# An attention and mixture-of-experts block: zeros multiplied on TensorE at the start, first loads reordered over two queues, a shorter first tile table, the last row copy issued later

## The reference

```
Q, K, V = x @ W_Q, x @ W_K, x @ W_V
x  = layernorm(x + softmax(causal(Q K^T / sqrt(128))) V)
logits = (x @ gate_w + gate_b) / 0.9 ; keep the best 2 of 8 ; p = softmax over those 2
h  = gelu(x @ w1[e] + b1[e]) ; y = sum over the 2 experts of p * (h @ w2[e] + b2[e])
x  = layernorm(x + (layernorm(y) * ln_g + ln_b))
```

## Time and profile before

| | us |
|---|---|
| median of 3 runs | 262.4 (260.68 to 263.1) |
| the profiled execution | 262.94 |
| its span in the trace | 261.1 |
| TensorE busy | 231.4 (89% of the span) |
| ScalarE busy | 179.9 (69%) |
| VectorE busy | 173.8 (67%) |
| GpSimd busy | 144.9 (55%) |
| mean granted TensorE clock | 0.963 of full |
| chain that ended last: TensorE, ScalarE, VectorE | 70%, 13%, 7% |

### The profile page before, as it was taken

How to read it: one execution, slowest core, us unless ns; L and a number is a source line. 1 busy time by engine, 2 the same in 40 slices (tenths; PEclk the granted TensorE clock), 3 DMA queues, 4 the chain that set the end, 5 groups by cost and what they waited for, 6 DMA issues and landing times.

```text
span 261.1 us, 7284 instructions
## 1 busy us (share of the span) xinstructions
PE 231.4 (89%) x1867; PEld 211.8 (81%) x1868; DVE 173.8 (67%) x957; ACT 179.9 (69%) x527; POOL 144.9 (55%) x165
## 2 busy tenths in 40 slices
PE   2789899899999899989999999999999999999200
PEld 2547687787887799989999999999999999999100
DVE  0043768688888878556883333355568989899984
ACT  2355675687784879968877655665566897589962
POOL 8300004727777777777877777766544445555600
PEclk9999999999999979999999999999999999999755
DMA  4999210221221345441527797768689775834266
GB/s 126 257 324 330 57 43 23 91 62 55 91 92 54 82 131 139 119 129 53 124 74 213 230 313 212 247 195 238 197 250 357 240 206 169 258 137 122 80 207 166
DMA packets 45105, 42.38 MB, mean 162 GB/s; under 512 B 5488, under 2 KB 34080, under 8 KB 45072
## 3 DMA queue, kind: packets, MB, share of 16 engines
q1 hardware_dynamic: 40752, 33.10, 44.4%
q0 software_dynamic: 4320, 8.92, 9.8%
HBM read 27.89 MB, written 12.01 MB: 153 GB/s over the span
## 4 chain that ended last, share of the span: by engine, by line
PE 70%; ACT 13%; DVE 7%; issue 3%; DMA 2%; DVEq 2%; SPq 1%; ACTq 1%
PE bank L584 21%; PE bank L573 21%; PE bank L434 6%; PE bank L461 6%; ACT h L737 4%; PE bank L420 3%; PE bank L501 3%; PE bank L449 2%; ACT pair L742 2%; PE bank L425 2%; PE bank L482 2%; ACT probs L665 2%; ACT rows L657 2%; DMA slot_x<-slots 2%; PE bank L581 1%
## 5 line engine op out<-in xcount | busy, mean ns | idle before, releaser
L737 ACT ACTIVATE h<-bank,b_cols 128x128 f32<-128x128 f32 x284 | 81.9, 383 | 38.3 <-PE bank L573 37.9
L1322 POOL DMA_INDIRECT slots<-rows,slot_of x64 | 65.4, 1022 | 57.1 <-DVE rows L972 38.8
L1327 POOL DMA_INDIRECT returned<-x,slot_back x71 | 71.4, 1006 | 44.4 <-DVE x L1107 35.2
L584 PE MATMUL bank<-w_all,h 128*128 x568 | 78.5, 282 | 0.0
L573 PE MATMUL bank<-slot_xT,w_now 128*128 128x128 f32 x568 | 75.0, 275 | 0.0
L584 PEld LDWEIGHTS bank<-w_all,h 128*128 128x128 f32 x568 | 69.0, 192 | 0.8
L573 PEld LDWEIGHTS bank<-slot_xT,w_now 128*128 128x128 f32 x568 | 69.1, 192 | 0.1
L869 DVE CAST slot_back<-slot_x 128x1 uint32<-128x1 f32 x71 | 10.4, 146 | 39.5 <-PE bank L573 39.5
L826 DVE TENSOR_REDUCE negmax<-bank 128x1 f32<-128x128 f32 (+3 forms) x32 | 14.7, 484 | 20.4 <-PE bank L435 19.9
L461 PEld LDWEIGHTS bank<-v,probsT 128*128 128x128 f32 x160 | 20.3, 198 | 5.7 <-issue 3.8
L1107 DVE TENSOR_SCALAR x<-bank,slot_gate 128x128 f32<-128x128 f32 x71 | 24.0, 341 | 0.0
(11 more groups left out here) (152 smaller groups left out, 305.5 us busy)
## 6 DMA issues: line engine op xcount, KB each, us to landing
w_now<-in_L_ffn_w_dram SPq DMA_DIRECT2D x47, 256.0 KB
slot_x<-slots SPq DMA_DIRECT2D x71, 65.0 KB
w_all<-in_L_ffn_w_dram SPq DMA_DIRECT2D x16, 256.0 KB, 5.8
pair<-returned SPq DMA_DIRECT2D x14, 256.0 KB, 4.2
x<-n_L_attn_embeddings_dram SPq DMA_DIRECT2D x8, 256.0 KB, 4.2
rows<-rows SPq DMA_DIRECT2D x8, 256.0 KB, 2.8
returned<-x,slot_back POOLq DMA_INDIRECT x71, 3.1
slots<-rows,slot_of POOLq DMA_INDIRECT x64, 2.3
```

The costliest lines, as they stand in the source:

```text
L584: m = nc.tensor.matmul(o, h[:, s % RING, c * P:(c + 1) * P], w2_c, start=False, stop=(c == FC - 1))
L737: m = nc.scalar.activation(h[:, s % RING, cols], bank_[:, cols], ACT.Gelu, bias=b1_cols[:, c:][:, bass.ds(first, 1)])
L1322: g_.indirect_dma_start(slots, bass.IndirectOffsetOnAxis(ap=slot_of[:, b, c:c + 1], axis=0), rows[:, k, b * TB + t, :], None).then_inc(dis ...
L1327: g_.indirect_dma_start(returned, bass.IndirectOffsetOnAxis(ap=slot_back[:, j:j + 1], axis=0), y[:, j % Y_RING, :], None).then_inc(y_retur ...
```

## The change

- A tile `idle` of 128 x 512 bf16 is set to zero as VectorE's first instruction. TensorE multiplies it (`stay_awake`, 128 x 128 by 512 columns) five times before its first wait for data, once after the m matmul and once after batch 0's projection. The products go to a bank that is written over later.
- x of batch 0 is issued from ScalarE's queue, as its first instruction. wq and wk are SyncE's first two DMAs. wv has a semaphore of its own, and TensorE waits for it only before the values of batch 0.
- ScalarE copies xT of batch 0 before mqk.
- Three operations on `taken` (one partition, eight numbers) move from the first table to the second.
- `copy_rows(7)` is issued after the load of slot 13 in place of slot 10.

```diff
+        idle = sb("idle", [P, 512], BF16)
...
-        w_loaded = sem("w_loaded")
+        idle_ready = sem("idle_ready")
+        w_loaded, wv_loaded = sem("w_loaded"), sem("wv_loaded")
...
-            load_x(0)
             sp.dma_start(wq[:], W_Q).then_inc(w_loaded, 16)
             sp.dma_start(wk[:], W_K).then_inc(w_loaded, 16)
-            sp.dma_start(wv[:], W_V).then_inc(w_loaded, 16)
+            sp.dma_start(wv[:], W_V).then_inc(wv_loaded, 16)
             load_x(1)
...
-                    if j == UNROLL + AHEAD - 1:
+                    if j == UNROLL + AHEAD + 2:
                         copy_rows(B - 1)
...
+            def stay_awake(n):
+
+                for _ in range(n):
+                    nc.tensor.matmul(T0[:], idle[:, 0:P], idle[:], start=True, stop=True)
+
+            pe.wait_ge(idle_ready, 1)
+            stay_awake(5)
             pe.wait_ge(const_ready, FIRST_CONST)
-            pe.wait_ge(w_loaded, 48)
+            pe.wait_ge(w_loaded, 32)
             nc.tensor.transpose(A1[:, 0:P], wq[:], ident[:])
             nc.tensor.transpose(A1[:, P:2 * P], wk[:], ident[:]).then_inc(wT_psum, 1)
             transpose_x(0)
             pe.wait_ge(wT_ready, 1)
             nc.tensor.matmul(A1[:, 2 * P:3 * P], wqkT[:, 0:P], wqkT[:, P:2 * P], start=True, stop=True).then_inc(m_psum, 1)
+            stay_awake(1)
             pe.wait_ge(m_ready, 1)
             project_g(0)
+            stay_awake(1)
+            pe.wait_ge(wv_loaded, 16)
             project_v(0)
...
+            act.dma_start(x[:, 0:TB, :], emb[0].rearrange("(t p) d -> p t d", p=P)).then_inc(x_loaded[0], 16)
             act.wait_ge(ones_ready, 1)
             nc.scalar.activation(egap[:, 0:1], ones[:, 0:1], ACT.Exp)
             act.wait_ge(wT_psum, 1)
             nc.scalar.activation(wqkT[:], A1[:, 0:2 * P], ACT.Copy).then_inc(wT_ready, 1)
+            copy_xT(0)
             act.wait_ge(m_psum, 1)
             nc.scalar.activation(mqk[:], A1[:, 2 * P:3 * P], ACT.Copy, scale=SCALE).then_inc(m_ready, 1)
-            copy_xT(0)
...
                 elif q == 4:
                     vec.tensor_tensor(some, tiles_by(FULL, E), by_tiles(ends[:, 0:E], FULL, E), ALU.is_ge)
-                    vec.tensor_tensor(taken[:], full[:], ends[:, 0:E], ALU.subtract)
                 elif q == 5:
                     vec.tensor_tensor(some, some, by_tiles(skip[:, 0:E], FULL, E), ALU.mult)
-                    vec.tensor_scalar(taken[:], taken[:], float(FULL * P), 0.0, ALU.add, ALU.max)
                 elif q == 6:
                     vec.tensor_reduce(steps[:, 0:FULL], some, AX.X, ALU.add)
-                    vec.tensor_tensor(taken[:], taken[:], full[:], ALU.min)
...
                     vec.tensor_copy(pad_at[:], running[0:1, B % 2, :]).then_inc(pads_known, 1)
+                    vec.tensor_tensor(taken[:], full[:], ends[:, 0:E], ALU.subtract)
...
                     vec.tensor_scalar(up_i[:], up[:], float(P - 1), None, ALU.add)
+                    vec.tensor_scalar(taken[:], taken[:], float(FULL * P), 0.0, ALU.add, ALU.max)
...
                     vec.tensor_scalar(up_i[:], up_i[:], -P, None, ALU.bitwise_and)
+                    vec.tensor_tensor(taken[:], taken[:], full[:], ALU.min)
...
+            vec.memset(idle[:], 0.0).then_inc(idle_ready, 1)
             vec.memset(both[:], 0.0)
```

## The result

| | before | changed |
|---|---|---|
| median of the runs compared | 262.75 us (260.68 to 265.95, 4 runs) | 257.81 us (257.17 to 258.35, 4 runs) |
| ratio | | 0.9847, interval 0.9804 to 0.9889 |
| profiled execution | 262.94 us, span 261.1 | 257.17 us, span 255.4 |

The ratio on record is estimated from fast executions alone (those over 1.5% above the fastest, here 265.95, do not count), so it is not the quotient of the two medians, which is 0.981.

The account below looks back on a forecast made before the run. TensorE, busy 89% of the span and partly at half clock, was taken as the bound. Gains 0.85 + 0.44 + 3.9 + 0.25 + 1.10 = 6.54 off the profiled 262.94 gave 256.4 us, range 254.2 to 259.2.

Parts of the forecast that it names:

- First loads: Kernel start: TensorE waits for wq and wk alone and begins at 3.75 instead of 4.59, gain 0.85 us (0.25 to 0.85).
- late bound of 2.9: Upper bound for wk's flight from issue to landing at the start; TensorE would then begin at 4.35, gain 0.25 us.
- Copy order: ScalarE in batch 0: xT is copied during the m matmul and only mqk follows, hiding 0.44 us.
- The zero product behind the m matmul: Single zero multiplication on TensorE in batch 0, estimated at 0.44 us, covered by ScalarE's copies and taken as costing 0.
- Clock: Batch 0 on TensorE: zeros from 1.3 bring the high clock at 6.8, scores end at 11.75; gain 3.9 us (3.3 to 4.2).
- Rival 1: Kernel start: clock rise counted from the end of the transposes, 5.25, so it comes at about 10.4; 257.9 us, chance 0.12.
- Tile table: VectorE's chain to the attention part's last normalisation: three one-partition operations leave it, gain 0.25 us (0 to 0.3).
- Row copy: Expert loop: slots 11 to 13 load before the last row copy, removing TensorE's wait for slot 11; gain 1.10 us at most.
- Slot 25: Expert loop: load needing all dispatches finished, issued at 136.26, wanted at 140.80; slack of 4.5 us shrinks to 3.4.
- rival 3: Expert loop: the removed stall is given back at slot 25, up to 1.1 us; 257.5 us, chance 0.12.
- rival 5: GpSimd during SyncE's padding writes: all last eight dispatches stretch, slot 25 comes 10.6 us later; 266.5 us, chance 0.03.
- rival 4: The clock's fall at 91.5 goes away as TensorE's pauses shrink and shift, worth 1.7 us; 254.7 us, chance 0.14.

## Why the prediction held, and where it was off

The time fell into the range with some luck. The measured parts of the profiles, 0.24 + 0.51 + 3.23 + 0.24 + 1.39, and 0.17 around the fall at 91.5, make 5.78 us against 6.54. Between medians it is 3 to 5 us, because the sum was taken off one execution; and the largest part, as far as one profile of each kernel can show, came by other edits than the one that it was credited to.

**First loads: too optimistic.** 0.85 was taken and 0.24 came. The step that failed is wk's flight of 2.3 us, held because "x was equally in flight when wk took 2.3". It wasn't: before, x had been issued 1.05 us ahead of wk and on the same queue, now 0.47 and on the other. The flight was 2.94, 3.02, 2.95, 3.08 and 3.15 in five profiles with this order (3.0 to 3.1 in the three others), past the late bound of 2.9, and 1.9 and 2.0 with both weights first. The lead alone does not explain it: before, wq went out 0.50 us behind x on x's queue and took 2.5; in the changed kernel wv went out 0.94 us behind x and took 2.8. Which of lead, queue and bytes in flight decides is open.

**Copy order: mechanism right, size 0.51 against 0.44.** The zero product behind the m matmul, costed at 0, is the last thing before the projection on the chain, but it ended within 0.06 us of mqk's copy (6.66). The order has a second effect that the sum left out: undone, it takes the early clock with it (0.4 to 0.5 us expected, 1.2 measured).

**Clock: 3.9 taken, 3.23 in the profile** (3.98 less 0.75), just under the lower end of 3.3. Here a nearly right number hides a wrong cause. The sum counted the rise from the first zero product at 1.3, but the kernel without zeros has the rise at 8.60 and, reckoned in the same way, 2.99 of the 3.23 in its profile, and the kernel with the zeros and the old copy order has it at 13.2. So the early rise came with the copy order, to which the sum gave nothing of it. The step's assumption that a short pause between zeros and transposes does no harm did not hold for the pause as it was, 0.77 us and not 0.3, because wk was late: in the four profiles with five zeros and this load order the pause was 0.77 to 0.98 and the rise at 7.91 to 13.2, while seven zeros without a pause gave 5.26, and the two kernels with both weights first, whose transposes follow the zeros at once, 6.02 and 5.0. Part of the miss is not the clock: the values of batch 0 take 1.13 us when fully warm, in the kernels with early rises too, where the sum had batch 1's 0.91. Rival 1 is refuted as a mechanism: forty transposes alone bring the rise. By its time (257.9) it would have looked right, 0.1 us from the median.

**Tile table: 0.25 taken, 0.24 measured** (3.98 to 4.22). This part is the firmest: from batch 1's projection to ScalarE's rows it takes 65.69 to 65.77 us in the four profiles with the old table, and 65.50 to 65.53 in the eight with the new one and no fall of the clock between.

**Row copy: 1.10 taken, 1.39 in the profile,** the restart behind the wait included. The mistake isn't the size but what it was taken for: a property of the kernel, when it was in one of three profiles. The same holds for the rise at 16.4. Parts that were peculiar to this execution cannot be gained in one that lacks them, so "262.94 minus the parts" overstated the gain over a median run. They don't explain its time, though: the other profile with 262.99 us had neither.

**Slot 25: misread, and rival 3 at a third of its price.** The prediction, like the caption of the earlier trace rows, took the load at 136.26 for tile 25's and gave it a slack of 4.5. It was slot 24's, which waits for the second tile table. Tile 25's, which waits for the dispatches, is the next, in the timelines of SyncE before and changed:

```profile
137.25 0.35 SPq L303 DMA_DIRECT2D slot_x<-slots  x1
```

```profile
132.65 0.35 SPq L305 DMA_DIRECT2D slot_x<-slots  x1
```

Before, it was wanted at 140.80, a slack of 3.55; in the changed kernel at 135.01, 2.36, and the rows came in time. In the two other profiles of before and with the row copy alone, where TensorE doesn't stand still at slot 11, it is 1.4 us nearer to both loads, and 0.14, 0.71 and 0.40 us went there (steps of 2.14, 2.71 and 2.40 against 2.00). The 0.71 belongs to slot 24 and so to the second tile table, not to the dispatches. Rival 3 had priced slot 25 at up to 1.1 with 0.12; its mechanism exists, outside the changed kernel's profile.

**Stretched dispatches (rival 5):** two of the last eight, as before, and not more.

```profile
120.38 2.46 POOL L1335 DMA_INDIRECT slots<-rows,slot_of  x1 [0.30 <-issue]
123.14 2.81 POOL L1335 DMA_INDIRECT slots<-rows,slot_of  x1 [0.30 <-issue]
```

The last dispatch ends at 131.00 instead of 135.53; the price of more stretched ones was not tried.

**The fall at 91.5: rival 4's event came, its price did not.** It was absent in the changed kernel and in both new profiles of before. But the shift grew by only 0.17 over that stretch, not by 1.7. Not even that is the fall's for certain, since from ScalarE's rows to tile 7's product the two other profiles of before, without the fall, took 24.71 and 24.56 us against 24.69 with it. Without the fall the chain there runs through VectorE's normalisation and ScalarE's rows (to 92.17 in the changed kernel), so TensorE had time in hand. The fall at 46, where the chain is TensorE from end to end, cost 1.65.

## What to carry to other kernels

A sum against one profiled execution takes over everything that was peculiar to that execution: profile the kernel before two or three times and see which waits and which clock changes are in each, before pricing their removal. Take warm-up work out again and look whether the early clock stays: here it did in the one profile taken, and was lost with the order of two copies. Warm-up work should reach into the real work: with a pause of 0.77 us or more behind five products no profile shows a gain from them. A slow-clock stretch of 3.4 us cost half its length where TensorE was the chain and nearly nothing where it was not: look at what released the next engine.

## What the runs showed of the hardware

- Products of zeros and float32 transposes each brought the high clock by themselves, with the clock record beginning at 6.64 (work since 1.26) and 6.44 (work since 2.57). The Trainium skill, "TensorE: Matmul & The Clock Gate", Part 4 (PE-mode transpose), says that transposes do not count as a busy engine in the same way; the trace with forty float32 transposes disagrees with it. No run here tries bf16 ones.
- The clock fell once for 3.4 us in some executions and not in others of the same kernel: at 91.5 in one of three profiles of before, at 46.1 in one of two of the changed kernel. The price was at most 0.17 and 1.65 us. What brings the fall is not shown.
- Of 64 KB loads issued at the very start, the first on a queue landed in 1.9 to 2.6 us, whichever queue; the second on its queue, with a 256 KB load from the other queue in flight, in 2.9 to 3.15. Behind the 256 KB load on one queue, as in the kernel before, the second and third landed in 2.2 to 2.5.
